# The loop over the middle slots of a four-layer graph kernel, written out as straight-line code

## The reference

```python
x = _layernorm(x + _L0(x, adj, adj, b))              # edge layer: adj @ x, row maximum, relu
x = _layernorm(x + _L1(x, W, a, beta, adj))          # graph attention: h = x@W, softmax(att)@h, elu
x = _layernorm(x + _L2(x, adj, weight, bias))        # adj @ x @ weight + bias
x = _layernorm(x + _L3(x, adj, Wq, bq, Wk, bk, Wv, bv))  # 8-head masked self-attention
```

## Time and profile before

| | |
|---|---|
| time, median of 3 (lowest to highest) | 2515.55 us (2514.35 to 2517.22) |
| time of the profiled execution | 2513.85 us |
| its span, first to last instruction | 2511.9 us |
| PE busy / weight loads busy | 97% / 82% of the span |
| DVE / POOL / ACT busy | 88% / 58% / 53% |
| granted TensorE clock, mean | 0.989 of full speed |
| mean DMA traffic | 136 GB/s |

### The profile page before, as it was taken

The page is one execution under the profiler, slowest core; times in us unless marked ns, Lnnn a source line. Parts: engine busy times, 40 slices in busy tenths (PEclk is TensorE's granted clock), DMA queues, the critical chain, the costliest instruction groups (busy, mean ns, idle before and its releaser), DMA issues. The chain is left out here.

```text
span 2511.9 us, 55083 instructions
## 1 busy us (share of the span) xinstructions
PE 2434.1 (97%) x15509; PEld 2072.2 (82%) x15509; DVE 2208.4 (88%) x6939; ACT 1333.6 (53%) x4104; POOL 1454.0 (58%) x1801
## 2 busy tenths in 40 slices
PE   3899999999999999999999999999999999999995
PEld 2788888888888888888888888888888888888884
DVE  5889889889889989999999999999999999999974
ACT  3455555555555555555555555555555555555543
POOL 2555566566566566566566566565565665665641
PEclk9999999999999999999999999999999999999997
DMA  4256666666666666666666666566666666666564
GB/s 131 64 131 138 140 139 139 141 139 140 140 139 140 139 139 140 139 139 142 138 138 142 138 138 142 138 138 142 138 140 140 139 141 138 141 139 139 126 139 101
DMA packets 1375069, 341.01 MB, mean 136 GB/s; under 512 B 1078576, under 2 KB 1339312, under 8 KB 1375024
## 3 DMA queue, kind: packets, MB, share of 16 engines
q1 hardware_dynamic: 1375024, 340.47, 59.5%
HBM read 173.35 MB, written 166.99 MB: 135 GB/s over the span
## 5 line engine op out<-in xcount | busy, mean ns | idle before, releaser
L929 PE MATMUL rot<-w_hi,y_hi 128*128 128x512 f32 x1024 | 415.5, 406 | 3.0 <-DVE y_lo L843 2.3
L931 PE MATMUL rot<-w_hi,y_lo 128*128 128x512 f32 x1024 | 403.6, 394 | 0.0
L930 PE MATMUL rot<-w_lo,y_hi 128*128 128x512 f32 x1024 | 402.0, 393 | 0.0
L506 ACT ACTIVATE probs<-score,sc_nmax 128x128 f32<-128x128 f32 x1024 | 362.1, 370 | 26.0 <-DVE sc_nmax L678 22.9
L380 POOL TENSOR_TENSOR ve<-mv,eps_col 128x1 f32<-128x1 f32 (+1 forms) x448 | 130.1, 291 | 350.9 <-DVE mv L663 256.4
L413 POOL TENSOR_TENSOR x2b<-x,bias 128x512 f32<-128x512 f32 x128 | 165.9, 1296 | 272.9 <-DVE x L782 272.9
L423 POOL TENSOR_SCALAR e<-e 128x512 f32<-128x512 f32 x128 | 246.9, 1929 | 24.0 <-ACT e L566 24.0
L678 DVE CUSTOM_DVE_ANT_0 score<-score,mask 128x128 f32<-128x128 f32 x1024 | 259.4, 315 | 1.3 <-PE score L1028 1.3
L388 POOL TENSOR_TENSOR rs<-ve,half_neg 128x1 f32<-128x1 f32 (+1 forms) x448 | 250.3, 572 | 0.6
L700 DVE CUSTOM_DVE_ANT_0 dot_tmp<-x,u 128x512 bf16<-128x512 f32 x256 | 234.3, 951 | 18.3 <-ACT x L615 13.7
L408 POOL TENSOR_TENSOR x<-x,o_norm 128x512 f32<-128x512 f32 x128 | 165.6, 1294 | 141.4 <-DVE o_norm L736 141.4
(11 more groups left out here) (129 smaller groups left out, 7036.5 us busy)
## 6 DMA issues: line engine op xcount, KB each, us to landing
pt_hbm<-probs SPq DMA_DIRECT2D x508, 128.0 KB, 2.8
probs_t<-pt_hbm SPq DMA_DIRECT2D x127, 512.0 KB, 4.0
x_in<-in_x SPq DMA_DIRECT2D x128, 256.0 KB, 4.0
xt_hbm<-x_b SPq DMA_DIRECT2D x512, 64.0 KB, 2.1
xt_f<-xt_hbm SPq DMA_DIRECT2D x128, 256.0 KB, 2.8
out_x<-x SPq DMA_DIRECT2D x128, 256.0 KB, 2.5
ot_hbm<-o_t SPq DMA_DIRECT2D x508, 64.0 KB, 1.9
o_norm<-ot_hbm SPq DMA_DIRECT2D x127, 256.0 KB, 2.7
```

What stands on the lines that cost most here:

```text
L506: ins = act.activation(probs[:, 0, c, t, :], score_tile(c, g, h), ACT.Exp, bias=sc_nmax[:, c, t:t + 1], scale=-1.0, accum_out=sc_sum[:, pa ...
L929: pe.matmul(outp, lh, rh, start=first, stop=False)
L930: pe.matmul(outp, lh, rl, start=False, stop=False)
L931: return pe.matmul(outp, ll, rh, start=False, stop=last)
```

## The change

The loop of 28 turns becomes 112 slots written out. The instructions of `emit` are the same and in the same order; the values waited for and the DRAM addresses become constants, and the loop's counter and branch go.

```diff
     for s in range(WARM):
         emit(Slot(s - s % BUFS, s % BUFS))
-    with eng.Fori(0, (LOOP_END - WARM) // BUFS) as turn:
-        for c in range(BUFS):
-            emit(Slot(turn * BUFS + WARM, c))
+    for s in range(WARM, LOOP_END):
+        emit(Slot(s - s % BUFS, s % BUFS))
     for s in range(LOOP_END, SLOTS):
         emit(Slot(s - s % BUFS, s % BUFS))
```

## The result

| | before | after |
|---|---|---|
| time, median (lowest to highest) | 2514.95 us (2514.01 to 2517.22) | 2541.10 us (2537.73 to 2544.57) |
| ratio, 95% interval | | 1.0103 (1.0085 to 1.012) |
| span of the profiled execution | 2511.9 us | 2542.7 us |

The change makes the kernel slower by 26 us, 1.0%. The forecast was 2538 us. Of all runs of this document one was disturbed, a run of e8 that took 3487.99 us at a mean granted clock of 0.655, and it stands outside e8's range and ratio.

What follows compares the result with a forecast made beforehand. PE was taken to bound the kernel, streaming matmuls without a gap in mid-loop. Band hits of 20.5 us plus 2.5 gave +23 on the 2511.9 us span; with 1.95 and 1.7 us more, 2538 us, range 2519 to 2566.

Steps and rivals of the forecast that it cites:

- The signs: New profile: PE waits for `probs_t` of 0.6 to 1.2 us in 20 to 30 even slots, unhit slots 18.79 us.
- The reason given for even slots: Stores ahead of the scatters leave even slots 0.4 to 0.6 us slack; in storeless slot 9 scatters still land in 2.6 us.
- The rival of no change: Packets delay the scatter too seldom or in harmless phases, or early waits were pipeline filling: 2514 to 2519 us, chance 0.14.
- that of faster: Branch and register work delay PE's or SP's next instructions, so PE runs on sooner without them: about 2513 us, chance 0.03.
- that of locking: The packets' phase does not drift out of the harmful band: 2560 to 2566 us, +45 to +50 us, chance 0.2.
- that of another engine running out of code: DVE, ACT or POOL reach the end of their loaded code and wait: 28 us, 2543 us, chance 0.05.
- The band: Packet times before PV, from -11 to about -5.5 us in even slots, at which PE waits.
- the price of a hit: PE's wait at PV when a packet falls in the band of an even slot: 0.89 us on average.
- The drift: Movement of the q8 packets' phase against the slots: -0.1 to -0.3 us a slot, possibly 0; -0.1 taken.
- The start: The packet's phase before PV from which the drift was counted: about -6.4 us in slot 14.
- 23 hits in the band: Even slots from 16 on hit before the phase leaves the band at drift -0.1: 23 x 0.89 = 20.5 us.
- 2.5 us for everything else: Added for q14 packets and stray hits in the gather, half of a few hits of 0.3 to 0.9 us.

Runs made afterwards that it cites:

- e8: Changed kernel with the two stores of a pair in slots 12 to 123 cut to one row of 128, the rest of that output left out: 2517.38 us.
- e3: Changed kernel plus 9 satisfied-wait instructions on PE in every odd slot of the 112, so two slots are two code packets: 2571.31 us, ratio 1.0231.
- e4: As e3, with 89 more such instructions at the start of PE's program, which moves all packets earlier: 2517.41 us, ratio 1.0008.
- e2: Kernel before, with only the 112 slots of DVE, ACT, POOL and SP written out and PE keeping its loop: 2521.03 us, ratio 1.0021.

## Why the prediction was right

**The mechanism.** Its core held: code packets delay the scatters of `probs`, and PE waits where the slot has no slack. The signs came as listed: waits at PV for `probs_t`, all but one (slot 117, 0.3 us) in even slots, in runs; slots without a hit at 18.79 us; no gain from the constants on any engine; landing of the scatters near 4 us at a hit. The reason given for even slots was in part wrong. The prediction read from slot 9 that a packet at the same place does no harm without the stores. But in an odd slot a packet near -6.7 comes after the scatters, whose last issue ends 8.1 us before PV; at -9.5, in slots 57, 59 and 115 of the changed kernel, it does delay them (last landed 4.5, 4.1 and 4.1 us before PV, in place of 5.9) and the slack covers it, as in e8. The rival of no change falls with e3 against e4, that of faster with the unchanged slot length, that of locking with the groups in the waits, and that of another engine running out of code by e2: its ten waits are all at PV.

**The band and the price of a hit.** The band from -11 to -5.5 us was right in its core: in slots 54 to 68 (phases -9.7 to -6.9) every even slot waits, 6.8 us / 8 = 0.85 us each, against 0.89 taken. In all 14 even slots of the band from 16 to 122 the mean is 0.96. Slots 46 to 52 at -12 wait for nothing.

**The drift, a step that failed.** The prediction had the phase move by -0.1 to -0.3 us a slot, "possibly 0". On the mean it moves by +0.33. The q8 packets from slot 54 (phase -9.7) to slot 112, which has nearly the same phase (window 1008 to 2111 us):

```profile
q8 instruction: 57, 0.93, 0.4%
```

57 packets in 58 slots: the phase goes once round, 18.8 us, in 57 slots. It does not move evenly, and that is why the packets of the earlier trace rows misled. It is -6.4 in slot 12 and -1.7 in slot 13, stays between -12.3 and -11.6 from slot 45 to 53, between -9.8 and -8.8 in most slots from 54 to 60, between -7.7 and -6.4 from 61 to 68, and is -1.8 in slot 69; in slots 16 to 122 none falls between -6.3 and -1.9. Three intervals within such a stay show next to nothing of the mean drift. Why it stays and jumps is open. The mean follows from the counts in the trace, 503 PE instructions in two slots or 251.5 a slot, against 256 a packet. The start was wrong too: in the changed kernel the packet of slot 14 is at -0.6, not at -6.4, and the 0.65 us wait of that slot, which the prediction let stand, is gone. The Trainium skill, Runtime: NRT & Kernel Launch, section "Instruction fetch mechanics", gives blocks of 16 KiB or 256 instructions, and the trace agrees (57 x 256 / 58 = 251.6 instructions a slot).

**The count of hits, and why the sum came out.** The prediction had 23 hits in the band, 20.5 us, and 2.5 us for everything else. In 212:2340 there are 28 waits of 22.6 us, against 2 of 1.8 before; 27 of them, 22.0 us, lie in slots 16 to 122. The band has 14 of these and not 23, 13.4 us in place of 20.5: 8 in slots 54 to 68 (6.8 us) and 6 in slots 112 to 122. The other 13, 8.6 us in place of 2.5, are the five at -14 us through the issue of `ot` on SP, which I had not seen (slots 40, 42, 44, 100, 102; 4.4 us), three at the lower edge of the band or in odd slot 117 (1.1 us), and five of 3.0 us in slots with an 8 KB packet 8 to 15 us before PV and no 16 KB packet near the scatters; e2, which has 8 KB packets alone, has seven such waits in these slots, 2.5 us. So the band's term was 7 us too large, that of the rest 6 us too small, and some 4.6 us of the 26.6 lengthen slots without being recorded as such a wait. That the median came within 3.1 us of the forecast is in part luck, two errors that cancel. An estimate: with the measured +0.33 a slot, and the prediction's own start, band and price, it would have had 14 or 15 hits, 13 us, and with its 2.5 us more some 2531 us.

**The rule that crossing a code block is hidden** (same section of the Trainium skill) held where no packet met the scatters, as in e4, and where the slack covered the delay, as in e8, and not in full even slots (e3, +56 us).

## What to carry to other kernels

A loop whose body is held is free of code loading (here one packet in 2063 us), and writing it out adds DMA packets that are negligible in bytes (0.6% of the engines here) but each of which took 1.1 us (median); if the kernel depends on a transfer with less slack than the delay that such a packet brings, the packets show up as waits wherever the phases meet. Before unrolling, look in the profile for the slack of the tightest transfer in each kind of slot and at the stretches that are already written out: they hold the collisions that the rest will have. A mean drift of the packets against the slots has to come from counts of instructions, not from a few intervals. Lengthening a loop's body past what is held was worse than either here (+50 us).

## What the runs showed of the hardware

A code packet of 16 KB among the four scatters of 128 KB made them land later, 4.3 us in place of 3.2 in slots 66 and 50 of the changed kernel; with the stores cut to one row (e8) it still made the last of them land 1.3 us later (5.8 and 4.5 us before PV). Where it met SP's issue of four scatters it stretched the issue from 1.94 to between 2.9 and 3.6 us; beside an 8 KB packet alone the median stayed at 1.94.

PE held a loop body of 1020 instructions (one q8 packet in 2063 us) and not one of 2034 (154 packets in the span); where between them the limit lies was not tried. Between e3 and e4, 89 instructions that did nothing, at the start of PE's program, changed the time by 54 us: the phase of code loading is part of a kernel's timing, and an edit that adds a few instructions to one engine can move it.
